# A fused attention and feed-forward block: the products of ones at two barriers are taken out

## The chip, the cores and the metric

The kernel runs on one core of one Trainium2 chip, as one program. The metric is the device time of one execution in microseconds; the median of several runs stands for a kernel. Four engines compute: PE (TensorE, products), DVE (VectorE), ACT (ScalarE) and POOL (GpSimd); SP issues most of the DMAs. PE's clock has two levels, 2.4 and 1.2 GHz; the profile gives the granted one as a share, 1.00 or 0.50.

## What is computed

x is 8 x 256 x 256, the context ctx has the same shape. All weights are float32.

```python
x = x + tanh(g_xattn) * attention(layernorm(x), ctx, ctx, Wq, Wk, Wv)
#   scores masked causally, softmax over the QUERY axis, values added up
x = x + tanh(g_ffn) * ffn(layernorm(x))

def act_fake_quant(x, clip):              # one scale for the whole tensor
    scale = sigmoid(clip) * max(abs(x)) / 127
    return clip(round(x / scale), -128, 127) * scale

def ffn(x):                               # hidden width 704
    xq = act_fake_quant(x, clip_x)
    h = silu(xq @ wq(w_gate).T) * (xq @ wq(w_up).T)
    return act_fake_quant(h, clip_down) @ wq(w_down).T
#   wq: the same rounding for weights, with one scale for each row
```

What matters here is `max(abs(x))` over the whole tensor, which stands in the block twice: no value can be quantised before the last one is known. These are the two barriers.

## The kernel before

It is written engine by engine, with semaphores between them; each engine works through its instructions in the order of the code, so the order on PE is the one in the text of the tensor block.

The program has three stages. In the first (to about 67 us) the eight batch entries go through attention one after the other; PE interleaves scores, queries, values and transposes of neighbouring entries (`scores`, `project_queries`, `values`, `attend`, `transposes2`). The last entry's pieces are written out at the end of the stage: attention products (L583 to L593), then `transposes2(LAST - 1)` (L502), then the first barrier.

The second stage multiplies the quantised x (`xq`) with the gate and up weights: five full slots of 128 hidden columns and one half slot. `hidden(i, half)` makes 8 products of 128x512 (L635) for each slot and half; ACT applies silu (L825) and copies the up half (L830), DVE and POOL multiply (L1091, L401), and DVE takes the running maximum (L1096). The half slot is L655, L843, L1114. Then PE turns the down weights (`turn_down`, L523) and the second barrier follows.

The third stage multiplies with the down weights, `down(c)` for eight pairs of row tiles (L682, L683, twelve products of 128x256 each). ACT makes integers (L851, L853, L860), DVE or POOL clips them into `hq` (L1141, L1148, L414), DVE scales and adds the residual (L1126, L1130, L1155, L1158), SP stores. `hq` has two buffers: POOL's clip for pair c waits for the down products of pair c - 2.

A barrier runs like this (`global_scale`): DVE reduces the partial maxima of each partition to one column `col_max` (L1047). PE spreads it over the partitions with one product against a diagonal, `spread_max` (L530). DVE takes the maximum of the row that comes out, `act_scale` (L1049), and its reciprocal `act_inv` (L1052). Then DVE, ACT and POOL make integers with it: L1059, L812, L815, L395 at the first barrier, L1135, L851, L853 at the second.

On PE, `keep_warm` (L428) stands around each spread. It multiplies `ones`, a float32 tile of 128x128, with itself into a bank that nobody reads, 6 products before and 7 behind the first spread, 15 before and 7 behind the second. At the first barrier four transposes (L603) of the last entry stand between the spread and the 7. Each float32 product is two passes, two records in the trace. `warm_up` (L423), eight products of a bfloat16 tile `dense` at the program's start, is another function. POOL sets `ones` at the start of the program (L330).

Of the kernel before, what the change touches and what calls it, by code (L numbers as in the profile page):

```python
# [17 lines left out]
P = 128  # L18
# [22 lines left out]
SCORE_SCALE = float(D) ** -0.5  # L41

WARM_AT_START = 8
WARM_BEFORE_MAX = 6
WARM_AT_BARRIER = 7
WARM_BEFORE_MAX2 = 15
FIRST_ACT_SLOTS = 6
SECOND_ACT_SLOTS = 7

# [1 line left out]
def gated_block(nc, x, xc_in, wq_in, wk_in, wvT_in, scalars_in, wgu_in, wd_in, out):  # L51
    assert S == 256 and D == 256 and REST == P // 2 and B == 8 and HALF == 2 * CH

    with ExitStack() as stack:
        def sb(name, shape, dt=F32):
            return stack.enter_context(nc.sbuf_tensor(name, shape, dt))

        def sem(name):
            return stack.enter_context(nc.semaphore(name))
# [21 lines left out]
        ident_bf = sb("ident_bf", [P, P], BF16)  # L81
        causal = sb("causal", [P, S])
        dense = sb("dense", [P, CH], BF16)
        ones = sb("ones", [P, P])
        minus_half = sb("minus_half", [P, QT])

        bnq = sb("bnq", [P, KT, 6])
# [61 lines left out]
        U, V0, V1, SC, AT, X2, RB, WT = range(8)  # L149
        VB = (V0, V1, WT, V0, V1, WT, V0, V1)  # L150

        def bank(n):
            return ps[:, n, :]
# [37 lines left out]
        wd_here = sem("wd_here")  # L191
        zeroed = sem("zeroed")
        rest_zeroed = sem("rest_zeroed")
        ones_set = sem("ones_set")
        dense_set = sem("dense_set")
        consts = sem("consts")
        tanh_done = sem("tanh_done")
# [129 lines left out]
        @block.gpsimd  # L327
        def _(pool):
            nc.gpsimd.memset(dense[:], 1.0).then_inc(dense_set, 1)
            nc.gpsimd.memset(ones[:], 1.0).then_inc(ones_set, 1)  # L330
            nc.gpsimd.memset(ident[:], 0.0).then_inc(zeroed, 1)
            nc.gpsimd.memset(causal[:], 0.0).then_inc(zeroed, 1)
            nc.gpsimd.memset(minus_half[:], -0.5).then_inc(consts, 1)
# [85 lines left out]
        def _(pe):  # L419
            def warm_up(products, bk):  # L420

                for _ in range(products):
                    nc.tensor.matmul(bank(bk), dense[:, 0:P], dense[:], start=True, stop=True)  # L423

            def keep_warm(products, bk):

                for _ in range(products):
                    nc.tensor.matmul(bank(bk)[:, 0:P], ones[:], ones[:], start=True, stop=True)  # L428

            def values_tile(b, k):  # L430
                weights = wvT_g if b == LAST else wvT
# [94 lines left out]
            def spread_max(n, bk):  # L526

                pe.wait_ge(clip_diag_done, 2)
                pe.wait_ge(col_max_done, n + 1)
                nc.tensor.matmul(bank(bk)[:, 0:P], col_max[:, n:n + 1].to_broadcast([P, P]), clip_diag[:, n, :],  # L530
                                 start=True, stop=True).then_inc(max_spread, 1)
# [11 lines left out]
            for e in range(KT):  # L543
                for h in range(KT):
                    last = nc.tensor.matmul(bank2(X2)[:, e, :], wq_c[:, h, e * P:(e + 1) * P], wk_sb[:, h, :],  # L545
                                            start=(h == 0), stop=(h == KT - 1))
# [47 lines left out]
                attn_done, 1)  # L594
            transposes2(LAST - 1)
            pe.wait_ge(x1_done, LAST)
            keep_warm(WARM_BEFORE_MAX, AT)
            spread_max(0, AT)
            pe.wait_ge(xn2_ready, B)
            pe.wait_ge(wguT_ready, 2)  # L600
# [3 lines left out]
                                               xn2[p][:, t, e * P:(e + 1) * P], ident[:])  # L604
            last.then_inc(tr2_done, 1)
            pe.wait_ge(x1_out, QT)
            keep_warm(WARM_AT_BARRIER, SC)


            pe.wait_ge(wguT_ready, 2)  # L610
# [49 lines left out]
            turn_down(0, 4)  # L660
            turn_down(1, 5)
            pe.wait_ge(up_out_done, FULL)
            keep_warm(WARM_BEFORE_MAX2, 6)
            spread_max(1, 7)
            keep_warm(WARM_AT_BARRIER, 6)


            def down(c):
# [533 lines left out]
```

## Time and profile before

| | |
|---|---|
| median of 3 runs | 116.38 us (116.06 to 116.40) |
| the profiled execution | 116.56 us, of which the span from the first to the last instruction is 114.7 us |
| PE busy | 103.8 us (91%) |
| DVE busy | 86.2 us (75%) |
| ACT busy | 69.9 us (61%) |
| POOL busy | 49.3 us (43%) |
| share of the chain that ended last | PE 58%, DVE 20%, POOL 8%, ACT 8%, issue 4% |

The busy time of PE includes the products of ones. Times in the rows are microseconds from the start of the span. A record of a product is longer than the distance to the next one, since products are pipelined; so for a run of products the distance is to be read, not the mean of a record. The chain is followed back from the last instruction, at each step to what released it.

### The profile page before, as it was taken

To read this page: it belongs to the slowest core of one execution; us is meant where nothing else is said; L and a number is where in the kernel's file an instruction comes from. 1 tells how busy PE (TensorE), PEld (TensorE's weight loads), DVE (VectorE), ACT (ScalarE), POOL (GpSimd) and SP (SyncE) were. 2 spreads that over 40 slices of the span, in tenths; PEclk is the share of its full clock that TensorE was granted. 3 is DMA by queue.
4 is the path that set the end of the run, shared out by engine and by line. 5 is a ranking of instruction groups with operands and counts; after the bars stand their busy time and mean duration, and the time that the engine had idled before them with its cause. 6 is when DMAs were issued, how large, how long until landed. Compare 5 with 4: busy or idle time off the path is not lost.

```text
span 114.7 us, 1828 instructions
## 1 busy us (share of the span) xinstructions
PE 103.8 (91%) x612; PEld 80.0 (70%) x612; DVE 86.2 (75%) x216; ACT 69.9 (61%) x129; POOL 49.3 (43%) x77
## 2 busy tenths in 40 slices
PE   5999797999999999999999669999999799879960
PEld 2488586988889888898999468444443498657740
DVE  0083454897998969768669968869999997888992
ACT  0403008567864576746887866599888861999600
POOL 7106050254270815424074384036687632198810
PEclk9999999999999999999999999999999999999997
DMA  3998999995000000000000000000000000023455
GB/s 78 362 358 216 390 419 425 412 411 230 0 0 0 3 0 0 6 0 0 0 3 0 0 0 9 0 0 0 0 0 0 6 0 0 0 91 127 161 174 183
DMA packets 5513, 11.65 MB, mean 102 GB/s; under 512 B 640, under 2 KB 2688, under 8 KB 5504
## 3 DMA queue, kind: packets, MB, share of 16 engines
q1 hardware_dynamic: 4784, 10.49, 24.8%
q10 hardware_dynamic: 720, 1.05, 2.7%
q8 instruction: 5, 0.08, 0.3%
q14 instruction: 4, 0.03, 0.1%
HBM read 9.44 MB, written 2.10 MB: 101 GB/s over the span
## 4 chain that ended last, share of the span: by engine, by line
PE 58%; DVE 20%; POOL 8%; ACT 8%; issue 4%; DVEq 0%; POOLq 0%; ACTq 0%
PE ps L455 12%; PE ps L433 12%; PE ps L481 9%; DVE hmax L1096 8%; POOL hq L414 4%; DVE shared L1091 3%; PE ps L682 3%; PE ps L423 3%; PE ps L491 2%; PE ps L502 2%; PE ps L635 2%; PE ps L493 2%; PE ps L492 2%; POOL shared L401 2%; PE ps L545 2%
## 5 line engine op out<-in xcount | busy, mean ns | idle before, releaser
L635 PE MATMUL ps<-xq,wguT 128*128 128x512 bf16 x80 | 17.4, 379 | 0.2 <-DVE xq L1064 0.2
L353 POOL TENSOR_TENSOR rstd<-var,minus_half 128x2 f32<-128x2 f32 x8 | 5.5, 693 | 25.5 <-DVE var L922 25.5
L401 POOL TENSOR_TENSOR shared<-up_sb,silu 128x1024 f32<-128x1024 f32 x5 | 11.8, 2363 | 10.0 <-ACT up_sb L830 10.0
L455 PE MATMUL ps<-shared,a_sb 128*128 128x256 f32 x64 | 15.1, 380 | 0.0
L433 PE MATMUL ps<-wvT,shared 128*128 128x256 f32 x56 | 14.6, 407 | 0.0
L635 PEld LDWEIGHTS ps<-xq,wguT 128*128 128x128 bf16 x80 | 7.7, 98 | 9.6 <-issue 0.7
L1096 DVE TENSOR_REDUCE hmax<-shared 128x1 f32<-128x2048 f32 (+1 forms) x6 | 12.7, 2108 | 0.6
L433 PEld LDWEIGHTS ps<-wvT,shared 128*128 128x128 f32 x56 | 11.3, 208 | 2.3 <-DMA shared<-in_xc 0.7
L825 ACT ACTIVATE silu<-ps,gu_scale 128x1024 f32<-128x1024 f32 x10 | 11.1, 1114 | 2.8 <-PE ps L635 2.8
L455 PEld LDWEIGHTS ps<-shared,a_sb 128*128 128x128 f32 x64 | 11.6, 191 | 1.3
L481 PE MATMUL ps<-uT,shared 128*128 128x256 f32 (+1 forms) x64 | 12.0, 330 | 0.6 <-DVE uT L881 0.6
L682 PE MATMUL ps<-wdT,hq 128*128 128x256 bf16 x80 | 10.9, 274 | 1.5 <-POOL hq L414 0.7
L481 PEld LDWEIGHTS ps<-uT,shared 128*128 128x128 f32 x64 | 10.4, 191 | 1.8 <-DVE uT L881 1.0
L682 PEld LDWEIGHTS ps<-wdT,hq 128*128 128x128 bf16 x80 | 7.2, 98 | 4.0 <-POOL hq L414 2.6
L414 POOL TENSOR_SCALAR hq<-ints 128x1408 bf16<-128x1408 int16 x6 | 8.2, 1359 | 3.4 <-ACT ints L860 2.7
L700 ACT COPY r_bc<-ps 128x256 f32<-128x256 f32 x8 | 3.0, 371 | 10.0 <-PE ps L465 10.0
L860 ACT ACTIVATE ints<-shared,act_inv 128x1408 int16<-128x1408 f32 x6 | 8.7, 1467 | 0.3
L428 PE MATMUL ps<-ones 128*128 128x128 f32 x70 | 8.5, 276 | 0.0
L428 PEld LDWEIGHTS ps<-ones 128*128 128x128 f32 x70 | 8.1, 192 | 0.0
L361 POOL TENSOR_SCALAR xn<-xs,neg_mean,rstd 128x256 f32<-128x256 f32 x14 | 7.7, 554 | 0.7
L720 ACT ACTIVATE vh<-ps,inv_sum 128x256 f32<-128x256 f32 x16 | 6.7, 470 | 2.0 <-DVE inv_sum L902 2.0
L705 ACT ACTIVATE probs<-neg_scores,neg_max 128x256 f32<-128x256 f32 x8 | 4.1, 509 | 5.9 <-DVE neg_max L893 5.9
(136 smaller groups left out, 204.4 us busy)
## 6 DMA issues: line engine op xcount, KB each, us to landing
shared<-in_xc SPq DMA_DIRECT2D x6, 512.0 KB, 10.2
out<-xs SPq DMA_DIRECT2D x7, 256.0 KB, 2.2
xs<-in_x SPq DMA_DIRECT2D x3, 512.0 KB, 8.4
shared<-in_wgu SPq DMA_DIRECT2D x3, 512.0 KB, 7.8
shared<-in_xc SPq DMA_DIRECT2D x3, 256.0 KB, 4.5
wd<-in_wd SPq DMA_DIRECT2D x1, 768.0 KB, 10.4
wvT<-in_wvT ACTq DMA_DIRECT2D x1, 256.0 KB, 3.8
wq_sb<-in_wq ACTq DMA_DIRECT2D x1, 256.0 KB, 4.8
```

The lines of the kernel that those rows point to most:

```text
L361: last = nc.gpsimd.tensor_scalar(xn2[b % 2][:, t, :], xs[:, QT * b + t, :], neg_mean[:, b, t:t + 1], rstd2[:, b, t:t + 1], ALU.add, ALU.mult)
L401: nc.gpsimd.tensor_tensor(hid[:, 2 * i + 1, :], up_sb[i % 2][:], silu1[i % 2][:], ALU.mult).then_inc(hid_done[1], 1)
L414: nc.gpsimd.tensor_scalar(hq[c % 2][:], hq_i16[c % 2][:], QMAX, -QMAX - 1, ALU.min, ALU.max).then_inc(hq_clipped, 1)
L428: nc.tensor.matmul(bank(bk)[:, 0:P], ones[:], ones[:], start=True, stop=True)
L433: last = nc.tensor.matmul(bank2(VB[b])[:, k, :], ctxT(b)[:, e, k * P:(k + 1) * P], weights[:, e, :], start=(e == 0), stop=(e == KT - 1))
L455: last = nc.tensor.matmul(query_bank(b, f), a_sb[:, e, f * P:(f + 1) * P], xT(b)[:, e, :], start=(e == 0), stop=(e == KT - 1))
L481: last = nc.tensor.matmul(bank(SC)[:, c0:c0 + n], ctxT(b)[:, f, k * P:(k + 1) * P], uT[b % 2][:, f, k * P:S], start=(f == 0), stop=(f == K ...
L635: last = nc.tensor.matmul(bank(4 * half + 2 * g + c), wguT[:, i, g, k, :], xq[:, k, col:col + CH], start=(k == 0), stop=(k == KT - 1))
L682: nc.tensor.matmul(dst, hq[c % 2][:, 2 * i + half, :], wdT[:, i, :], start=(i == 0), stop=False)
L825: nc.scalar.activation(dst[:], ps[:, 4 * half:4 * half + 2, :].rearrange("p c n -> p (c n)"), ACT.Silu, scale=gu_scale[:, i, 0:1]).then_in ...
L860: nc.scalar.activation(hq_i16[c % 2][:], hid[:, :, c * P:(c + 1) * P], ACT.Copy, scale=act_inv[:, 1:2]).then_inc(hq_int_act, 1)
L1096: nc.vector.tensor_reduce(hmax[:, n:n + 1], hid[:, first:first + count, :].rearrange("p s n -> p (s n)"), AX.X, ALU.max, apply_absolute_va ...
```

## The change

`keep_warm` and its four calls go, with the four numbers of products (three constants), the tile `ones`, its memset on POOL and the semaphore `ones_set`. `warm_up` and all waits stay.

```diff
-WARM_BEFORE_MAX = 6
-WARM_AT_BARRIER = 7
-WARM_BEFORE_MAX2 = 15
-        ones = sb("ones", [P, P])
-        ones_set = sem("ones_set")
             nc.gpsimd.memset(dense[:], 1.0).then_inc(dense_set, 1)
-            nc.gpsimd.memset(ones[:], 1.0).then_inc(ones_set, 1)
             nc.gpsimd.memset(ident[:], 0.0).then_inc(zeroed, 1)
-            def keep_warm(products, bk):
-
-                for _ in range(products):
-                    nc.tensor.matmul(bank(bk)[:, 0:P], ones[:], ones[:], start=True, stop=True)
             transposes2(LAST - 1)
             pe.wait_ge(x1_done, LAST)
-            keep_warm(WARM_BEFORE_MAX, AT)
             spread_max(0, AT)
...
             pe.wait_ge(x1_out, QT)
-            keep_warm(WARM_AT_BARRIER, SC)
...
             pe.wait_ge(up_out_done, FULL)
-            keep_warm(WARM_BEFORE_MAX2, 6)
             spread_max(1, 7)
-            keep_warm(WARM_AT_BARRIER, 6)
```

## Rows read from the trace of the kernel before

**Rows 1.** The page: granted clock in 40 slices, in tenths; shares of the chain

```profile
...
PEclk9999999999999999999999999999999999999997
...
PE 58%; DVE 20%; POOL 8%; ACT 8%; issue 4%; DVEq 0%; POOLq 0%; ACTq 0%
```

**Rows 2.** Line L428: records, duration ns min/median/max, first and last start

```profile
...
L428 PE MATMUL ps<-ones x70: 274/276/329, 67.4 to 97.6; 128*128 128x128 f32 x70
```

**Rows 3.** First barrier, in order of time: start us, us, engine, line

```profile
...
66.93 0.66 PE L502 MATMUL ps<-ident,xn 128*128 128x128 f32 x4 [1.93 <-POOL xn L361]
...
67.42 1.50 PE L428 MATMUL ps<-ones 128*128 128x128 f32 x12
...
67.86 0.16 DVE L1047 TENSOR_REDUCE col_max<-xmax 128x1 f32<-128x9 f32 x1
...
68.76 0.39 PE L530 MATMUL ps<-clip_diag,col_max 128*128 128x128 f32 x2
...
68.98 0.60 PE L603 MATMUL ps<-ident,xn 128*128 128x128 f32 x4
69.19 0.29 DVE L1049 TENSOR_REDUCE act_scale<-ps 128x1 f32<-128x128 f32 x1 [1.16 <-PE ps L530]
...
71.38 2.97 PE L635 MATMUL ps<-xq,wguT 128*128 128x512 bf16 x13 [0.23 <-DVE xq L1064]
```

**Rows 4.** Second barrier and first down products, the same view

```profile
...
91.46 0.84 PE L523 MATMUL ps<-ident_bf,wd_q 128*128 128x128 bf16 x12
...
92.14 3.57 PE L428 MATMUL ps<-ones 128*128 128x128 f32 x30
...
95.59 0.16 DVE L1047 TENSOR_REDUCE col_max<-hmax 128x1 f32<-128x6 f32 x1
...
95.90 0.46 PE L530 MATMUL ps<-clip_diag,col_max 128*128 128x128 f32 x2 [0.19 <-DVE col_max L1047]
...
96.40 0.29 DVE L1049 TENSOR_REDUCE act_scale<-ps 128x1 f32<-128x128 f32 x1 [0.64 <-PE ps L530]
...
98.38 0.71 PE L682 MATMUL ps<-wdT,hq 128*128 128x256 bf16 x5 [0.45 <-DVE hq L1141]
...
100.89 0.27 PE L683 MATMUL ps<-wdT_rest,hq 128*128 128x256 bf16 x1
```

**Rows 5.** Stretches: us, then each engine's busy time, granted clock, DMA

```profile
...
65.00:66.90 1.90, 0.00 (x0) 0.00 (x0) 1.63 (x7) 1.55 (x4) 1.80 (x5) 1.00 0.00 0
110.90:111.00 0.10, 0.04 (x1) 0.00 (x0) 0.10 (x2) 0.00 (x0) 0.00 (x0) 1.00 0.99 338
112.90:113.00 0.10, 0.00 (x0) 0.00 (x0) 0.00 (x0) 0.00 (x0) 0.00 (x0) 1.00 1.01 348
113.05:113.10 0.05, 0.00 (x0) 0.00 (x0) 0.00 (x0) 0.00 (x0) 0.00 (x0) 0.50 0.52 164
```

**Rows 6.** Start of the program, by line as rows 2: L423, then L433 at 6.1 and 7

```profile
...
L423 PE MATMUL ps<-dense x8: 606/635/635, 1.3 to 4.3; 128*128 128x512 bf16 x8
...
L433 PE MATMUL ps<-wvT,shared x2: 634/634/635, 5.7 to 6.1; 128*128 128x256 f32 x2
...
L433 PE MATMUL ps<-wvT,shared x3: 380/381/508, 7.0 to 7.5; 128*128 128x256 f32 x3
```

**Rows 7.** The page, costliest groups, L635: us busy, mean ns of one

```profile
...
L635 PE MATMUL ps<-xq,wguT 128*128 128x512 bf16 x80 | 17.4, 379 | 0.2 <-DVE xq L1064 0.2
```

**Rows 8.** The chain that ended last, in order of time: start us, us, what

```profile
...
75.18 1.12 ACT up_sb L830
...
100.48 1.37 POOL hq L414
...
102.73 0.55 PE ps L682 x5
```

**Rows 9.** POOL at the start, in order of time, with its idle time before

```profile
...
1.18 0.20 POOL L330 MEMSET ones<- 128x128 f32 x1
...
8.73 0.19 POOL L346 TENSOR_SCALAR var<-mv 128x2 f32<-128x2 f32 x1 [5.34 <-DVE mv L875]
```

## The prediction

> **What bounds the kernel now.** I read the page first: its clock line (PEclk) and the chain that ended last. The clock line is full until the last slice [rows 1]: TensorE ran at its upper level (2.4 GHz) whenever there was work. The chain gives PE 58% of the span [rows 1], but for the stages around this change that average says little. So next come the two stretches around the barriers (the places where one maximum over everything must be known before the next stage can start), in the view of instructions in order of time [rows 3, 4]. In each, the chain runs: last partial maximum on DVE (L1047), spread over the partitions by PE (L530), scale on DVE (L1049), then integers on DVE and ACT, then the first product of the next stage (L635, L682). PE has almost no work of its own here. What fills it is the ones: 70 records [rows 2], that is two passes for each of the 6+7+15+7 = 35 products that go away. Last come the rows that tell what the clock does when PE has nothing to do: the end and the start of the program [rows 5, 6].
>
> **What the change takes out, part by part.**
>
> *The ones ahead of the first maximum stand in the way.* col_max starts at 67.86 us, but the spread starts only at 68.76, behind twelve passes that run from 67.42 [rows 3]. At the second barrier the same pair of steps has no queue before it: col_max starts at 95.59, the spread at 95.90, the scale at 96.40 [rows 4]: 0.81 us from first to last. Put at the first barrier that gives 67.86 + 0.81 = 68.67 for the scale, where it now starts at 69.19 [rows 3]. Gain: 0.52 us. Is something else late then? The transposes L603 need POOL's last xn, and the pause they leave is not on the chain: the integers on DVE start right after the scale. I count the 0.52 us in full; if the transposes got in the way, some 0.1 of it would go.
>
> *The ones ahead of the second maximum are not in the way.* The thirty passes start at 92.14 and last 3.57 us, to 95.71 [rows 4], before col_max is even done (95.59 + 0.16). Removing them gives nothing.
>
> *The ones behind each spread are not in the way either.* Fourteen passes from 69.42 for 1.73 us end at 71.15; the first gate product starts at 71.38, released by DVE [rows 3]. With that release 0.52 us earlier they would have been; they are gone, so the gain stands. At the second barrier they end at 97.93 and the down products start at 98.38 [rows 4]. Zero.
>
> *The constant.* The memset of ones takes 0.20 us on POOL at 1.18; POOL later sits idle for 5.34 us before 8.73 [rows 9]. Nothing on the path gets its 0.2 us. 35 x 2 passes less to fetch and issue I also set at zero: PE's issue wasn't what ended a wait on the chain, bounds -0.1 to +0.1.
>
> *What goes with the ones is their cover of the clock.* This decides the sign. What rows show of it: the last product of the program ended at 110.94, and with PE idle the clock was 1.00 up to 113.00 and 0.50 from 113.05 [rows 5], so it fell to 1.2 GHz after 2.1 us of pause. A pause of 1.9 us (PE busy 0.00 in 65.00 to 66.90 [rows 5]) between full stretches did not make it fall. Without the ones, the pause before the second maximum goes from the end of the transposes L523, 91.46 + 0.84 = 92.30, to 95.90: 3.6 us, well past the 2.1 that was enough at the end. After 0.46 us of spread comes another pause of 2.0 us, 96.36 to 98.38. So I expect the lower clock when the down products start.
>
> *Price of the lower clock, per product.* At the start, eight products of 512 columns began between 1.3 and 4.3 us, one every 0.43 us (3.0 over 7 steps) [rows 6]. At full clock eighty take 17.4 us [rows 7], 0.218 each. So a product takes twice as long, and a stretch of T us at the low clock, kept full, leaves PE T/2 behind. The down products are 256 columns wide, 0.11 each (five in 0.55) [rows 8], so about 0.21.
>
> *How long it stays low.* The trace has one rise only. PE worked from 1.3 on; the products of L433 still took 634 ns at 6.1 and 380 a little after 7.0 [rows 6]: some 5.9 us of work until the clock rose. That is the upper end; the lower is zero (the clock is back with the first product). I take two thirds, 3.9 us, since the only row is at the upper end. PE falls 3.9/2 = 1.95 us behind over the first two pairs of row tiles.
>
> *Slack in the down stage.* PE isn't the bound there. Its second pair ends at 100.89 + 0.27 = 101.16 [rows 4], and what waits for it, POOL's next clip, starts at 100.48 + 1.37 = 101.85 [rows 8] because POOL and ACT are busy till then. So 0.7 us of lag costs nothing. The rest, 1.25 us, moves the chain of POOL clip, PE, POOL clip [rows 8], which has no pause to give it back. The spread itself at the low clock: 0.46 us now [rows 4] for two passes. Neither end is shown; between 0 and another 0.46, I take 0.2 (half of it: part of a record is fixed). Second barrier: 1.25 + 0.2 = +1.45 us. With 0 us of low clock it would be 0 to +0.2; with 5.9 us, 2.95 - 0.7 + 0.2 = +2.45.
>
> *Does the clock also fall at the first barrier?* After the change PE has, from 65.0: pause 1.9, transposes 0.66 (L502), pause 0.6 (67.59 to about 68.17), spread and transposes to about 69.2, pause 1.7 to about 70.86. No pause is over 2.1 us, but only 1.7 of 5.9 us are work. I hold a stay slightly likelier, because no single pause reaches the one that was enough at the end, and one of 1.9 us did no harm.
>
> The Trainium skill speaks against that, on its page "TensorE: Matmul & The Clock Gate", Part 4 (PE-mode transpose): a transpose doesn't count as activity for the clock in the way that a product does. No row of this case shows what they count for. By that rule the clock would fall here, and the time would be that of the first rival below.
>
> **Sum.** The profiled execution took 116.56 us (span 114.7, and 1.86 around it, which the change doesn't touch); the median of the three runs is 116.38, 0.18 less, and I add the changes to the median. -0.52 (first barrier) + 1.45 (second) = +0.93: **117.3 us**. With its own bounds (low clock for 0 to 5.9 us) this case goes from 115.9 to 118.3.
>
> **Rivals.**
>
> *The clock falls at both barriers.* For it: two thirds of the stretch from 65.0 to 70.9 is pause, and if the transposes L502 and L603 (0.66 and 0.60 us [rows 3]) don't keep the clock up, 0.46 us of spread is all that does. Against: the 1.9 us pause now, which does no harm with transposes right behind it. Price: the first gate products run at the low clock. The chain goes through the sixteen products of the first group to ACT's copy of the up half at 75.18 [rows 8]; sixteen at 0.218 from 71.38 end at about 75.0, so 0.2 us is slack. With 3.9 us: 1.95 - 0.2 + 0.2 (slow spread) = +1.95 us, less 0.52 = +1.4. DVE then works almost without a pause to the second barrier, so nothing is given back. With 1.45 at the second: 119.3; with half of 5.9 at each, 118.3. I put it at 118.8.
>
> *The clock stays up at both* (the other side: faster). Mechanism: the spread's two passes, and whatever PE does while it waits, are enough; place: 92.3 to 98.4. It decides if the clock still reads 1.00 at 98.4. Then only the gain is left: 116.38 - 0.52 = 115.86. Against it: 2.1 us of pause was enough at the end, and here it is 3.6.
>
> *The gain at the first barrier is eaten*, by the transposes L603 or a slower release of the spread, and the second costs what I said: 117.8.
>
> **Chances.** Forecast 0.44; both fall 0.36; stays up 0.10; gain eaten 0.10. About 0.3% (0.35 us) is what a measurement of this kernel can tell from no change. Faster by more than that: 0.10 from the third case and 0.02 from the forecast's lower end (clock back at once, so that PE's lag stays inside the slack): 0.12. Within: 0.13, all from the forecast's lower part, where the low clock lasts up to 2.7 us (2.7/2 - 0.7 + 0.2 - 0.52 = +0.33). Slower: 0.75. The range takes in most of the both-fall case and the lower end of the forecast, without the whole of the stays-up case: 116.0 to 119.2.
>
> **What the profile after would show.** First barrier: scale L1049 about 0.8 us after the start of col_max; if 1.3, the gain was not made. Clock row: 1.00 up to 92 and 0.5 when the down products start; 0.5 between 68 and 75 is the both-fall case, with records of L635 longer than their 379 ns of now [rows 7]. Down stage: the first twelve products twice as far apart, POOL's clips waiting for PE instead of ACT. The forecast is wrong if the low clock, once there, ends much sooner or later than 3.9 us after the first product, or if it starts at the first barrier too.

## The result, and the profile after

The changed kernel takes 119.03 us (median of 4 executions, 118.76 to 119.65) against 116.39 us before (4 executions, 116.06 to 117.81). The ratio is 1.024 (95% interval 1.019 to 1.030): 2.6 us slower. Ratios, here and below, leave out executions more than 1.5% above the fastest of their kernel, such as the 117.81, while medians hold all. The profiled execution took 119.65 us, its span is 117.9 us; before it was 116.56 and 114.7, so the two profiles differ by 3.1 us. That is more than the medians do, and the profiles are compared with each other below.

The page's clock line, 40 slices in tenths, shows two dips where [rows 1] has none:

```profile
...
PEclk9999999999999999999999985599999995589999
```

The same in stretches around the four edges of the dips (columns: stretch, its length, PE's busy time with the number of records, granted clock, DMA share, GB/s). A mean between 0.50 and 1.00 places the edge inside the stretch: 0.83 in the third column from the end puts the fall at 69.66, 0.76 the rise at 76.48, 0.98 the second fall at 96.96, and 0.60 the second rise at 103.80.

```profile
...
69.00:70.00 1.00, 0.22 (x3) 0.83 0.00 0
76.00:77.00 1.00, 1.00 (x5) 0.76 0.00 0
96.00:97.00 1.00, 0.00 (x0) 0.98 0.00 0
97.00:98.00 1.00, 0.01 (x1) 0.50 0.00 0
103.00:104.00 1.00, 1.00 (x8) 0.60 0.00 0
```

So PE ran at 1.2 GHz twice, 6.8 us each time. These places and the prices below are those of one execution: a second profile of the same kernel, further down, has two dips of the same length at other places.

First barrier, in order of time (start us, us, engine, line), to be held against [rows 3]. The line numbers are those of the changed file: L491 was L502, L519 L530, L1032 and L1034 L1047 and L1049, L622 L635, L815 L830.

```profile
...
67.80 0.16 DVE L1032 TENSOR_REDUCE col_max<-xmax 128x1 f32<-128x9 f32 x1
...
68.11 0.46 PE L519 MATMUL ps<-clip_diag,col_max 128*128 128x128 f32 x2 [0.59 <-DVE col_max L1032]
...
68.61 0.29 DVE L1034 TENSOR_REDUCE act_scale<-ps 128x1 f32<-128x128 f32 x1 [0.64 <-PE ps L519]
...
72.03 0.15 PEld L622 LDWEIGHTS ps<-xq,wguT 128*128 128x128 bf16 x1 [0.28 <-issue]
72.46 0.15 PEld L622 LDWEIGHTS ps<-xq,wguT 128*128 128x128 bf16 x1 [0.28 <-issue]
...
77.24 1.11 ACT L815 ACTIVATE up_sb<-ps,gu_scale 128x1024 f32<-128x1024 f32 x1
```

The scale (L1034) now starts 0.81 us after col_max, at 68.61 instead of 69.19: the gain ahead of the spread is there, and nothing else took its place. Then the weight loads of the gate products come every 0.43 us instead of every 0.22 [rows 7], and ACT's copy of the up half, at 75.18 before [rows 8], starts at 77.24: 2.06 us late. The first gate product started at about 70.8: its weights were loaded at 70.77 and its own record is missing from the trace, as is one more of the 80.

Second barrier and first down products, to be held against [rows 4] (L512 was L523, L667 and L668 L682 and L683, L408 L414):

```profile
...
97.69 0.16 DVE L1032 TENSOR_REDUCE col_max<-hmax 128x1 f32<-128x6 f32 x1
...
97.99 0.77 PE L519 MATMUL ps<-clip_diag,col_max 128*128 128x128 f32 x2 [3.59 <-DVE col_max L1032]
98.80 0.29 DVE L1034 TENSOR_REDUCE act_scale<-ps 128x1 f32<-128x128 f32 x1 [0.95 <-PE ps L519]
...
100.78 1.23 PE L667 MATMUL ps<-wdT,hq 128*128 128x256 bf16 x5 [2.01 <-DVE hq L1126]
...
103.66 1.36 POOL L408 TENSOR_SCALAR hq<-ints 128x1408 bf16<-128x1408 int16 x1 [3.44 <-PE ps L668]
```

col_max starts 2.10 us later than before (97.69 against 95.59), so the gate stage kept what it had lost and lost no more. The spread takes 0.77 us instead of 0.46, and the scale is 2.40 us late. The first five down products take 1.23 us instead of 0.71. POOL's clip for the third pair, which started at 100.48 because it waited for ACT [rows 8], now starts at 103.66 and waited 3.44 us for PE. The span ends 3.2 us later: 2.1 us come from the first barrier, 0.3 us from the slow spread and 0.8 us from the down products.

In the groups of the page the mean of a gate product goes from 379 ns [rows 7] to 419:

```profile
...
L622 PE MATMUL ps<-xq,wguT 128*128 128x512 bf16 x78 | 19.8, 419 | 2.0 <-DVE xq L1049 2.0
```

| step, start in us | before | after | difference |
|---|---|---|---|
| first scale (L1049, L1034) | 69.19 | 68.61 | -0.58 |
| ACT's copy of the up half | 75.18 | 77.24 | +2.06 |
| second col_max | 95.59 | 97.69 | +2.10 |
| second scale | 96.40 | 98.80 | +2.40 |
| first down product | 98.38 | 100.78 | +2.40 |
| end of the span | 114.7 | 117.9 | +3.2 |

### The profile page after: what moved, and what is told of

Same layout as the page of the kernel before. It is cut to its first block, busy times and chain, and to the rows that moved or that the text cites. A ratio compares the mean times of both kernels' runs of the same rounds, so it can differ in the third digit from the quotient of the medians.

```text
span 117.9 us, 1686 instructions
## 1 busy us (share of the span) xinstructions
PE 99.8 (85%) x540; PEld 72.9 (62%) x542; DVE 86.3 (73%) x216; ACT 70.0 (59%) x129; POOL 49.2 (42%) x76
## 4 chain that ended last, share of the span: by engine, by line
PE 57%; DVE 19%; POOL 7%; DMA 5%; ACT 4%; issue 4%; SPq 1%; POOLq 0%; DVEq 0%; ACTq 0%
PE ps L444 12%; PE ps L470 9%; PE ps L422 9%; PE ps L622 7%; DVE hmax L1081 6%; PE ps L667 5%; DMA shared<-in_xc 5%; POOL hq L408 3%; PE ps L480 2%; PE ps L482 2%; PE ps L481 2%; DVE shared L1076 2%; POOL shared L395 2%; PE ps L491 2%; PE ps L534 1%
## 5 line engine op out<-in xcount | busy, mean ns | idle before, releaser
L622 PE MATMUL ps<-xq,wguT 128*128 128x512 bf16 x78 | 19.8, 419 | 2.0 <-DVE xq L1049 2.0
L622 PEld LDWEIGHTS ps<-xq,wguT 128*128 128x128 bf16 x80 | 8.5, 106 | 13.1 <-issue 5.0
L667 PE MATMUL ps<-wdT,hq 128*128 128x256 bf16 x80 | 12.4, 296 | 2.3 <-DVE hq L1126 2.0
L422 PE MATMUL ps<-wvT,shared 128*128 128x256 f32 x56 | 13.6, 382 | 0.8 <-DMA shared<-in_xc 0.8
L422 PEld LDWEIGHTS ps<-wvT,shared 128*128 128x128 f32 x56 | 10.3, 190 | 3.2 <-DMA shared<-in_xc 2.0
L667 PEld LDWEIGHTS ps<-wdT,hq 128*128 128x128 bf16 x80 | 7.9, 106 | 5.6 <-issue 2.3
L408 POOL TENSOR_SCALAR hq<-ints 128x1408 bf16<-128x1408 int16 x6 | 8.2, 1359 | 4.3 <-PE ps L668 4.3
L1076 DVE SCALAR_TENSOR_TENSOR shared<-ps,gu_scale,silu 128x1024 f32<-128x1024 f32 x5 | 6.4, 1278 | 4.2 <-ACT silu L810 2.5
L892 DVE SCALAR_TENSOR_TENSOR xs<-ps,tanh_g,xs 128x512 f32<-128x512 f32 x7 | 5.2, 748 | 3.1 <-PE ps L482 3.1
```

Source lines behind the costliest of these rows:

```text
L408: nc.gpsimd.tensor_scalar(hq[c % 2][:], hq_i16[c % 2][:], QMAX, -QMAX - 1, ALU.min, ALU.max).then_inc(hq_clipped, 1)
L422: last = nc.tensor.matmul(bank2(VB[b])[:, k, :], ctxT(b)[:, e, k * P:(k + 1) * P], weights[:, e, :], start=(e == 0), stop=(e == KT - 1))
L622: last = nc.tensor.matmul(bank(4 * half + 2 * g + c), wguT[:, i, g, k, :], xq[:, k, col:col + CH], start=(k == 0), stop=(k == KT - 1))
L667: nc.tensor.matmul(dst, hq[c % 2][:, 2 * i + half, :], wdT[:, i, :], start=(i == 0), stop=False)
L1076: nc.vector.scalar_tensor_tensor(out=hid[:, 2 * i, :], in0=ps[:, 2:4, :].rearrange("p c n -> p (c n)"), scalar=gu_scale[:, i, 1:2], in1=si ...
```

## Experiments

The theory after this result: the ones hold PE's clock up, and each barrier's ones do so for the stage behind it. The main rivals are that one barrier is the cause of both, and that only one group of the four does the work while the others are there for nothing.

One thing about the numbers has to be said first. The kernel before itself comes in two kinds of executions: of 76 that ran beside these experiments, 45 took 116.07 to 116.67 us with a mean granted clock of 0.992 or more, and 31 took 117.29 to 118.25 us with 0.985 or less. A median depends on how many of either it holds, so for each kernel I give that count too: "low" means executions with a mean clock of 0.985 or less. The ratios compare with the kernel before on the same chip.

### One barrier at a time

```diff
-            keep_warm(WARM_BEFORE_MAX, AT)
             spread_max(0, AT)
...
-            keep_warm(WARM_AT_BARRIER, SC)
```

> The change at the first barrier alone: 6 + 7 products of ones out, the 15 + 7 at the second kept. Theory (each barrier's ones keep the clock up for its own next stage): low clock from about 69.7 to 76.5, the gate stage's first sixteen products at twice their distance, the second barrier as before; +2.1 us, 118.5 us. Rival (the clock at the second barrier is lost because the first one was disturbed): the clock falls at both, 119.0 to 119.6. Rival (the loss is in the second barrier alone): 115.9.

Measured: 118.52 us (118.01 to 119.00), against 116.46; ratio 1.013 (1.004 to 1.023); low in 4 of 4. The clock line has only the first dip:

```profile
...
PEclk9999999999999999999999975599999999999999
```

The median is 2.06 us up, but two of the four executions spent 2.5 and 2.7 us outside the span, where the others spent 1.8. The spans, 116.2 to 116.5 us against 114.3 to 114.7 for the kernel before at full clock, say 1.8 us. In the profile the second col_max comes 1.7 us later behind the first than before, where the changed kernel's profile has 2.1; the dip lies at 68.5 to 75.4, earlier than the 69.7 to 76.5 that I expected.

```diff
-            keep_warm(WARM_BEFORE_MAX2, 6)
             spread_max(1, 7)
-            keep_warm(WARM_AT_BARRIER, 6)
```

> The change at the second barrier alone: 15 + 7 products of ones out, the 6 + 7 at the first kept. Theory: full clock through the gate stage, low clock from some point of the 3.6 us pause until about 3 us after the first down product; spread 0.3 us slower; +1.1 us, 117.5 us (116.9 to 118.3 by when the clock comes back). Rival (needs the first to fall too): 116.4.

Measured: 118.24 us (117.91 to 119.65), ratio 1.015 (1.005 to 1.024); low in 4 of 4. Only the second dip:

```profile
...
PEclk9999999999999999999999999999999996569999
```

So each barrier loses on its own, and the rivals of both experiments are out. The median is above the 117.5 us that I wrote down, and inside its range; one execution took 119.65 us, at a mean clock of 0.942, as low as with both barriers bare. In the profile the spread ran at full clock (0.46 us), and the low clock lasted from 96.7 to 103.5, 5.4 us past the first down product instead of 3.

### One group at a time

The six ahead of the first spread are those that stood on the path.

```diff
-            keep_warm(WARM_BEFORE_MAX, AT)
             spread_max(0, AT)
```

> Only the 6 products ahead of the first spread are out. Theory A (the 7 behind the spread and the transposes are enough, the longest pause is 1.9 us): clock up all through, scale 0.5 us earlier, 115.9 us. Theory B (the share of work from 65 to 71 decides, and it goes from some 4.2 of 6.4 us to some 3.4 of 5.9): the clock falls at the first barrier in some or all executions, 117.5 to 118.5.

Measured: 116.85 us (115.78 to 117.45), ratio 1.000 (0.995 to 1.005); low in 9 of 10. Theory B holds in what it says of the clock: it fell in nearly all executions. It's wrong in the price. In order of time:

```profile
...
67.58 0.16 DVE L1046 TENSOR_REDUCE col_max<-xmax 128x1 f32<-128x9 f32 x1
...
67.89 0.77 PE L530 MATMUL ps<-clip_diag,col_max 128*128 128x128 f32 x2 [0.59 <-DVE col_max L1046]
...
68.69 0.29 DVE L1048 TENSOR_REDUCE act_scale<-ps 128x1 f32<-128x128 f32 x1 [0.95 <-PE ps L530]
...
69.30 2.54 PE L428 MATMUL ps<-ones 128*128 128x128 f32 x14
...
71.57 0.42 PEld L634 LDWEIGHTS ps<-xq,wguT 128*128 128x128 bf16 x3
```

The scale starts at 68.69, later than the 68.39 that 67.58 + 0.81 would give: the spread itself took 0.77 us at the low clock. The fourteen passes behind it now last 2.54 us, and they end at 71.8. In the kernel before they took 1.73 us:

```profile
...
69.42 1.73 PE L428 MATMUL ps<-ones 128*128 128x128 f32 x14
```

The first gate product's weights are loaded only at 71.57, so now the seven stand in its way. But in that time the clock came back (1.00 from 71.0 on), so the gate products ran at full speed. The one execution in which the clock held took 115.78 us, the time of the forecast gain.

This kernel and the one with the whole first barrier bare differ only by the seven behind the spread. With them the nine low executions have a mean clock of 0.985 and spans of 114.5 to 115.6 us, without them 0.966 to 0.971 and 116.2 to 116.5. So the seven, though they stand in the way, make the dip shorter (3.4 us in the one profile, 6.8 in the other) and save more than 1 us.

The seven behind the first spread:

```diff
             pe.wait_ge(x1_out, QT)
-            keep_warm(WARM_AT_BARRIER, SC)
```

> Only the 7 products behind the first spread are out; the 6 ahead of it stay, with their 0.5 us on the path. Theory (PE's share of work between 65 and 71 us decides; it goes from 4.2 of 6.4 us to some 2.5 of 6.4, between the kernel before and the change): low clock at the first barrier in most executions, 117.5 to 118.5 us. Rival (no pause is longer than 1.9 us, so it stays up): 116.4.

Measured: 116.55 us (116.25 to 118.49), ratio 1.003 (0.999 to 1.008); low in 4 of 10, beside 10 of 31 for the kernel before on that chip. The theory expected most executions low; they are not. With the six in place the seven can't be shown to do anything here; without the six they are worth over 1 us, as the pair above shows.

The fifteen ahead of the second spread:

```diff
-            keep_warm(WARM_BEFORE_MAX2, 6)
             spread_max(1, 7)
```

> Only the 15 products ahead of the second spread are out: the pause of 3.6 us is open, the 7 behind the spread stay. Theory: the clock falls in or right after that pause, the 7 run at the low clock and bring it back sooner than without them; spread up to 0.3 us slower, about half of the loss of the whole second part: 116.9 to 117.5 us. Rival (the 7 hold it up): 116.4.

Measured: 117.22 us (116.58 to 119.19), ratio 1.004 (0.998 to 1.009); low in 9 of 10. PE in the profiled execution, behind a pause of 3.6 us:

```profile
...
96.35 2.55 PE L428 MATMUL ps<-ones 128*128 128x128 f32 x14
98.69 1.27 PE L681 MATMUL ps<-wdT,hq 128*128 128x256 bf16 x5
...
99.97 0.95 PE L681 MATMUL ps<-wdT,hq 128*128 128x256 bf16 x5
...
100.87 0.71 PE L681 MATMUL ps<-wdT,hq 128*128 128x256 bf16 x5
```

The seven take 2.55 us for fourteen passes instead of 1.73, then the first down products 1.27 us for five and, from the second pair on, 0.71: the clock was back at 100.5. The seven don't hold it up, they are the work that runs at the low clock in place of down products. Here too the pair with the bare barrier shows what they are worth: 3.4 us of low clock in the profile instead of 6.8, and 117.22 us instead of 118.24 (on two chips, where the kernel before took 116.41 and 116.46). The interval of the ratio alone doesn't tell this from no change, the clock does.

The seven behind the second spread:

```diff
             spread_max(1, 7)
-            keep_warm(WARM_AT_BARRIER, 6)
```

> Only the 7 products behind the second spread are out: a pause of 2.0 us, 96.4 to 98.4, right behind 3.6 us of full work. Theory: as in the pause of 1.9 us ahead of the transposes at 66.9 the clock stays up in most executions: 116.4 us. Rival (a pause of 2.1 us was enough at the end of the program): low clock for the down products, 117.3 to 117.6.

Measured: 117.14 us (116.08 to 117.88), ratio 1.002 (0.997 to 1.007); low in 6 of 10. The profile shows where:

```profile
...
68.00:68.50 0.50, 0.50 (x6) 0.87 0.00 0
68.50:69.00 0.50, 0.50 (x5) 0.50 0.00 0
...
71.50:72.00 0.50, 0.50 (x6) 0.71 0.04 16
98.00:99.00 1.00, 0.00 (x0) 1.00 0.00 0
...
100.00:101.00 1.00, 1.00 (x12) 1.00 0.00 0
```

The pause of 2.0 us behind the second spread left the clock at 1.00. The dip, 68.4 to 71.8, lies at the first barrier, where this kernel is the kernel before. No low execution of the kernel before was profiled, so this profile is the nearest that there is to one:

```profile
...
67.57 2.03 PE L428 MATMUL ps<-ones 128*128 128x128 f32 x12
...
68.01 0.16 DVE L1046 TENSOR_REDUCE col_max<-xmax 128x1 f32<-128x9 f32 x1
...
69.39 0.63 PE L530 MATMUL ps<-clip_diag,col_max 128*128 128x128 f32 x2
...
70.06 0.29 DVE L1048 TENSOR_REDUCE act_scale<-ps 128x1 f32<-128x128 f32 x1 [1.89 <-PE ps L530]
```

The clock falls while the six are running. Twelve passes take 2.03 us instead of 1.50 [rows 3], and the spread stands behind them: its scale starts 2.05 us after col_max, at 70.06 instead of 69.19. In this execution the six cost the path 1.2 us, not 0.5. That the low executions of the kernel before are of this kind is likely, but not shown; nor is where the other five low executions of this kernel dipped.

### What counts, and where it has to stand

```diff
-                for _ in range(products):
-                    nc.tensor.matmul(bank(bk)[:, 0:P], ones[:], ones[:], start=True, stop=True)
+                for _ in range(2 * products):
+                    nc.tensor.transpose(bank(bk)[:, 0:P], ones[:], ident[:])
```

> The kernel before with each product of ones replaced by two transposes of the same tile (one pass each, some 0.11 us): the same passes at the same places, 70 in all. If a transpose keeps the clock up as a product does: the clock as before, 116.4 us. If it does not count (the rule of the Trainium skill): the clock falls at both barriers, with the 0.5 us on the path kept, 119.2 us or more.

Measured: 116.37 us (116.09 to 117.67), ratio 0.997 (0.992 to 1.001); low in 1 of 10. The records at L428 (duration min/median/max, first and last start):

```profile
...
L428 PE MATMUL ps<-ident,ones x70: 272/273/278, 67.4 to 97.6; 128*128 128x128 f32 x70
```

Seventy transposes hold the clock as seventy passes of products did. If they didn't count, nine of ten executions wouldn't have come in at full clock. Each transpose is one record, where a float32 product is two. So on this kernel the transposes are as good as products, and what the prediction draws from the page "TensorE: Matmul & The Clock Gate" (the Trainium skill, Part 4, PE-mode transpose), that a transpose doesn't count as activity in the same way, isn't borne out.

The next kernel keeps all 35 products and moves the six to the front of the pause of 1.9 us that PE has before the transposes, where nothing waits for it:

```diff
+            keep_warm(WARM_BEFORE_MAX, U)
             transposes2(LAST - 1)
             pe.wait_ge(x1_done, LAST)
-            keep_warm(WARM_BEFORE_MAX, AT)
             spread_max(0, AT)
```

> The 6 products stand ahead of the transposes of the last entry but one, in PE's pause of 1.9 us, instead of ahead of the spread; nothing is left out. Theory: twelve passes of 0.11 us end at about 66.4, before the transposes start at 66.9, so the scale comes 0.5 us earlier and the clock stays up: 115.9 us. Rival (it falls all the same, since the pause before the spread is open): 117.5 or more.

Measured: 115.79 us (115.54 to 116.02, 10 executions), ratio 0.993 (0.990 to 0.996); low in none of 10, beside 7 of 19 for the kernel before on that chip. It is faster than the kernel before by 0.7%, with the interval clear of 1, and so than the changed kernel.

```profile
...
64.53 1.50 PE L428 MATMUL ps<-ones 128*128 128x128 f32 x12
...
66.63 0.66 PE L502 MATMUL ps<-ident,xn 128*128 128x128 f32 x4 [0.59 <-POOL xn L361]
...
67.56 0.16 DVE L1047 TENSOR_REDUCE col_max<-xmax 128x1 f32<-128x9 f32 x1
...
67.87 0.46 PE L530 MATMUL ps<-clip_diag,col_max 128*128 128x128 f32 x2 [0.58 <-DVE col_max L1047]
...
68.36 0.29 DVE L1049 TENSOR_REDUCE act_scale<-ps 128x1 f32<-128x128 f32 x1 [0.64 <-PE ps L530]
```

The twelve passes start at 64.53 and last 1.50 us, to 66.03; the transposes start at 66.63, as soon as POOL releases them; the scale comes 0.80 us after col_max. And the clock line is full:

```profile
...
PEclk9999999999999999999999999999999999999999
```

Its gain has two parts. Against the executions of the kernel before at full clock on that chip (116.15 to 116.53, median 116.35) it is about 0.56 us, the part of the path that the six held. The rest of the 0.67 between the medians is that no execution had a dip.

Can the sevens go then?

> As few products of ones as the runs so far leave: the 6 moved into the pause of 1.9 us ahead of the transposes L502, the 15 ahead of the second spread kept, both groups of 7 out; 21 products instead of 35. Theory (the two long pauses are what the ones must fill, 64.9 to 66.9 and 92.3 to 95.9; the pauses of 1.7 to 2.0 us behind the spreads lie next to full work): clock up in nearly all executions, 115.8 us. Rival (the 7 are needed once the 6 stand earlier): some executions with the low clock at the first barrier, 116.5 to 118.

Measured: 117.68 us (116.13 to 121.02), ratio 1.006 (1.001 to 1.011); low in 9 of 10. On that chip the kernel before was low in 8 of 13, with a median of 117.38, so the count alone says little; but four executions took 118.2 to 121.0 us, and none of the kernel before was over 117.9. Its profiled execution was the one at full clock, so it can't say where the others lost. Two more kernels split it.

> The 6 moved into the pause at 65 us, the 7 behind the first spread out, both groups at the second barrier kept. If the low clock of the kernel with 21 products lay at the first barrier: 116.9 to 117.8 us in most executions here. If it lay at the second: 115.8 here.

Measured: 117.38 us (115.68 to 118.27); low in 3 of 4. The dip is at the first barrier:

```profile
...
69.00:70.00 1.00, 0.04 (x1) 0.93 0.00 0
70.00:71.00 1.00, 0.01 (x1) 0.50 0.03 8
...
73.00:74.00 1.00, 1.00 (x5) 0.87 0.00 0
```

> The 6 moved into the pause at 65 us, the 7 behind the first spread kept, the 7 behind the second spread out. If the low clock of the kernel with 21 products lay at the first barrier: 115.8 us here. If it lay at the second (the pause of 2.0 us ahead of the down products): 116.5 to 117.8 in most executions here.

Measured: 115.93 us (115.52 to 116.39), ratio 0.992 (0.988 to 0.996); low in 4 of 10. In the profiled execution the dip is at the second barrier:

```profile
...
97.00:98.00 1.00, 0.62 (x5) 0.88 0.00 0
98.00:99.00 1.00, 1.00 (x7) 0.50 0.00 0
101.00:102.00 1.00, 1.00 (x11) 0.91 0.00 0
```

It begins at 97.8, 0.4 us past the end of the pause of 2.0 us (95.37 to 97.38), and ends at 101.2. The four low executions took 116.29 to 116.39, the others 115.52 to 116.01: 0.6 us between their means. Neither of the two times that I had written down came out. So the seven behind the first spread are needed once the six stand earlier: without them three of four executions took 117.0 to 118.3, with them none over 116.4 on the same chip. Those behind the second are worth 0.6 us in some executions. Against the kernel before, this last kernel (0.992) can't be told from the one with all 35 and the six moved (0.993); the other two are worse.

### The changed kernel once more

> The changed kernel once more, to see how it spreads over more executions beside the single parts. Theory (both barriers lose on their own and add up: +2.1 and +1.1 to +1.8): 118.8 to 119.7 us in every execution, none near 116.4. Rival (by where the pauses fall in an execution the clock sometimes holds at the first barrier): some executions between 116.8 and 117.8.

Measured: 119.09 us (118.86 to 119.34), ratio 1.015 (1.010 to 1.021) on a chip where the kernel before was low in 8 of 13 executions (median 117.38); low in 4 of 4. The changed kernel hardly moved between the two measurements (119.03 and 119.09), the kernel before did. Against its executions at full clock (116.34 to 116.67) the change costs 2.7 us, against its low ones (117.31 to 117.89) 1.6.

Its profiled execution (118.86 us, span 117.1) has two dips again, but at other places:

```profile
...
PEclk9999999999999999999999855999999996579999
```

```profile
...
66.00:67.00 1.00, 0.53 (x3) 0.81 0.00 0
73.00:74.00 1.00, 1.00 (x5) 0.78 0.08 16
97.00:98.00 1.00, 0.02 (x1) 0.67 0.00 0
104.00:105.00 1.00, 1.00 (x10) 0.92 0.74 254
```

```profile
...
66.47 1.02 PE L491 MATMUL ps<-ident,xn 128*128 128x128 f32 x4 [1.94 <-POOL xn L355]
...
70.71 1.86 PE L622 MATMUL ps<-xq,wguT 128*128 128x512 bf16 x4 [1.37 <-DVE xq L1049]
...
99.04 1.22 PE L667 MATMUL ps<-wdT,hq 128*128 128x256 bf16 x5 [2.02 <-DVE hq L1126]
```

Read as above, the first lasts from 66.6 to 73.4 and the second from 97.3 to 104.2, 6.8 us each. The first begins 0.15 us behind the pause of 1.94 us, before any later pause has come. So it takes in the first spread (0.77 us) and only 2.7 us of gate products; the second begins after its spread (0.46 us) and takes in 5.1 us of down products. What the first barrier costs and what the second costs changes with where the dip falls: from the first col_max to the second it was +2.16 us in the first profile and +1.12 in this one, from the second col_max to the end +1.1 and +1.7.

## Why the prediction was wrong

119.03 us lies inside the range of 116.0 to 119.2, and slower was right. But the forecast of 117.3 us gave the change 0.93 us, and it cost 2.6. It was the first rival, both barriers, at 118.8 us, that came true. The range holds the result because it took in most of that rival, not because the forecast's account was right.

**The step that failed: does the clock also fall at the first barrier.** I held a stay slightly likelier because none of the pauses (1.9, 0.6 and 1.7 us) reached the 2.1 us of the end of the program. It fell in both profiles of the changed kernel, at 69.7 and at 66.6, in that of the first barrier alone at 68.5, and all four executions of the latter, whose second barrier still has its ones, were low. The argument took the 2.1 us of the program's end as what a single pause needs, and the pause of 1.9 us as harmless because one profile had the clock up behind it. What the runs show is a clock that falls with no pause over 1.95 us: in one execution 0.15 us behind that very pause, in the others in or behind a later one, with up to 1.1 us of work in between. Whether the pauses add up or each has its own chance of doing it, these runs don't separate; filling the first was enough only with the seven behind the spread in place. With the six ahead of the spread the low count was 31 of 76, without them 9 of 10, with them moved to 65 us none of 10. My own sum (1.7 us of work in 5.9) stood in the text and pointed to this.

**The price of both barriers together was about right; by stage it isn't a fixed number.** With 3.9 us of low clock at each stage my own terms give 116.38 + 1.43 + 1.45 = 119.3 us, and 119.03 and 119.09 were measured. The length past the first gate product was 5.7 us in one profile (70.8 to 76.5) and 2.7 in the other, where I took 3.9. With 5.7 the sum gives 5.7/2 - 0.2 = 2.65 less the gain of 0.58: +2.07, and the profile has +2.06. With 2.7 it gives 2.7/2 - 0.2 + 0.3 - 0.5 = +0.95, and the profile has +1.1. So the formula holds to 0.2 us there. The slow spread, for which I had added 0.2 here, came only where the clock fell before or during the spread.

**The gain was right.** 0.52 was forecast, 0.58 measured, of which 0.06 was there before the barrier (col_max at 67.80 instead of 67.86). The kernel with the six moved confirms it: 0.56. Where the clock falls before the spread, as in the second profile, 0.3 us of it is lost again: the scale comes 1.11 us after col_max.

**Second barrier.** The fall was right, and so was its cause, the pause of 3.6 us: opening it alone made 9 of 10 executions low. In one profile the clock fell inside it, at 96.96, and the spread cost 0.31 where I took 0.2; in the three others with this pause open it fell 0.3 to 0.6 us behind a spread at full clock. From the first down product to the rise it was 3.0 us (100.8 to 103.8), where I took 3.9; 3.0/2 - 0.7 + 0.3 = +1.1, and the profile has 3.2 - 2.1 = +1.1. My +1.45 was too much by 0.35. In the second profile it was 5.1 us, 5.1/2 - 0.7 = +1.85, where the stage took 1.7 us longer. In the kernel without ones at the second barrier alone it was 5.4 us, 5.4/2 - 0.7 = +2.0, where its stage took 1.7 us longer (from col_max at 95.32 to the end at 116.1, against 95.59 to 114.7). So the slack of 0.7 us is right to 0.3.

**The zeros.** The fifteen and the two sevens stood in nobody's way, as forecast, at full clock. At the low clock they do: in the kernel without the six, fourteen slow passes held up the gate products. And with the six or the fifteen gone, each seven saves more than it costs.

**The rivals.** A clock that stays up fell with every execution of the changed kernel. "The gain is eaten" fell too.

**The base.** I took 116.38 us as the time of one kind of execution. The three executions that I had, 116.06 to 116.40, were all of the faster kind, and so was the profile; a fourth in the comparison took 117.81. That the first barrier loses the clock in some executions even with all its ones could not be read from them, and it would have told me that this barrier has nothing to spare.

What stays open: why the same instructions keep the clock in one execution and lose it in the next. The profile without the seven behind the second spread and that of the kernel before have the same instructions at the same distances up to the fall, 0.15 us apart. The traces show when it fell, not why then.

## What to carry to other kernels

Look for a stage start ahead of which the engine with the gated clock has been mostly idle, and don't call it safe because its longest pause did no harm in one profile: here the clock fell behind one of 1.94 us. Work that only keeps the clock up belongs into a pause that ends before the critical step is released, not in front of that step: here the move alone gave 0.7%, and leaving out all 35 products cost 2.4%. A dip costs by what it covers, so two executions of one kernel can lose in different stages. And look at the clock of several executions of the kernel before, since one profile at full clock doesn't say that every execution is.

## What the runs showed of the hardware that I had not expected

- The same program has executions with and without a dip of the clock: 31 of 76 for the kernel before, 117.3 to 118.3 us instead of 116.1 to 116.7.
- The eleven dips that the profiles place lasted either 6.8 us (two in each profile of the changed kernel; 68.5 to 75.4 and 96.7 to 103.5 with one barrier bare) or 3.4 us (67.6 to 71.0 and 97.1 to 100.5 without the six and without the fifteen; 68.4 to 71.8 with the first barrier's ones in place; 69.9 to 73.3 and 97.8 to 101.2 with the six moved and one seven out).
- Transposes of a float32 tile held the clock as float32 products did (1 low execution of 10, beside 10 of 31).
- A pause of 2.0 us between full stretches left the clock up in one profile (97.8 to 99.8, without the seven behind the second spread) and was followed by a fall 0.4 us later in another (at 97.8, with the six moved as well). The pause of 1.94 us ahead of the transposes did the same: up in the kernel before, a fall at 66.6 in the changed one.
- The granted clock of the profile reads 1.00 from the start of the span, though the products there stood at twice their distance up to 7 us [rows 1, 6]: the level before the first change isn't in the row. My sentence that TensorE was at its upper level whenever it had work was wrong for that stretch.
